# Attention and routed experts on one core: routing spread behind its batches, tables in four stages, first tile asked for earlier

## What is computed

```python
x = x + xattn(layernorm(x), ctx, ctx, Wq, Wk, Wv, Wo, bo)     # softmax(q k / 4) v Wo + bo
gate = softmax(layernorm(x) @ w_gate.T)                        # 8 experts
topk_scores, topk_idx = top_k(gate, 2)
h = gelu(einsum('td,edh->teh', ln_x, W1) + b1)
y = einsum('teh,ehd->ted', h, W2) + b2
x = x + einsum('ted,te->td', y, cw)                            # cw: the two scores, else 0
```

## Time and profile before

| | us |
|---|---|
| median of 3 runs | 514.05 (508.76 to 515.09) |
| span of the profiled execution | 496.2 |
| TensorE busy | 446.2 (90%) |
| VectorE busy | 361.9 (73%) |
| ScalarE busy | 324.5 (65%) |
| GpSimd busy | 179.4 (36%) |

### The profile page before, as it was taken

One profiled execution on the slowest core, in us unless ns is written; L12 is line 12 of the kernel. 1 busy time (PEld: TensorE's weight loads), 2 busy tenths in 40 slices (PEclk: granted clock), 3 DMA queues, 4 the chain that ended last, 5 costly groups with the idle time before them and its releaser, 6 DMA issues.

```text
span 496.2 us, 10173 instructions
## 1 busy us (share of the span) xinstructions
PE 446.2 (90%) x3585; PEld 373.5 (75%) x3585; DVE 361.9 (73%) x784; ACT 324.5 (65%) x521; POOL 179.4 (36%) x220
## 2 busy tenths in 40 slices
PE   5797989999998987858889989999999999999992
PEld 3354666767666664538889989999898898998982
DVE  4456776777777764546978997698789788797871
ACT  2133677667756633546969875898778879778860
POOL 5144340452620288701362505245321224212313
PEclk9799999999999976766999999999999999999997
DMA  7676624334122022367375999697797988977823
GB/s 235 189 208 191 205 85 155 109 127 139 66 91 85 26 77 91 131 218 306 135 239 187 282 286 248 231 281 246 227 264 234 273 259 256 279 257 243 282 37 36
DMA packets 44624, 93.19 MB, mean 188 GB/s; under 512 B 6990, under 2 KB 30350, under 8 KB 38684
## 3 DMA queue, kind: packets, MB, share of 16 engines
q1 hardware_dynamic: 35340, 81.56, 49.9%
q0 software_dynamic: 7152, 9.46, 9.6%
q10 hardware_dynamic: 2080, 1.49, 1.0%
HBM read 63.10 MB, written 14.32 MB: 156 GB/s over the span
## 4 chain that ended last, share of the span: by engine, by line
PE 55%; issue 10%; POOL 10%; DMA 8%; DVE 8%; ACT 5%; SPq 2%; ACTq 1%; DVEq 0%; POOLq 0%
PE bank L1380 14%; PE S L1344 10%; POOL lists L617 5%; PE bank L1447 5%; PE S L1357 5%; PE S L1479 4%; DVE nmax L940 3%; POOL x2n L607 3%; PE bank L1430 3%; DMA w_in<-in_W 3%; PE bank L1514 2%; PE bank L1439 2%; DMA lists<-zero 2%; PE bank L1422 2%; PE S L1502 2%
## 5 line engine op out<-in xcount | busy, mean ns | idle before, releaser
L576 POOL DMA_INDIRECT out<-y,slot x39 | 74.0, 1898 | 160.7 <-DVE y L848 87.4
L940 DVE TENSOR_REDUCE nmax<-S 128x4 f32<-128x1024 f32 x64 | 78.3, 1224 | 48.2 <-PE S L1479 45.5
L1344 PE MATMUL S<-xgT,Q 128*128 128x256 f32 x512 | 97.1, 289 | 3.2 <-DVE xgT L816 3.2
L1254 ACT ACTIVATE prob<-S 128x1024 f32<-128x1024 f32 x64 | 65.7, 1027 | 28.1 <-PE S L1502 26.4
L1344 PEld LDWEIGHTS S<-xgT,Q 128*128 128x128 f32 x512 | 79.9, 192 | 3.6 <-issue 2.5
L1158 ACT ACTIVATE hf<-S,b1c 128x256 f32<-128x256 f32 x128 | 53.2, 467 | 31.2 <-PE S L1344 30.6
L793 DVE TENSOR_TENSOR K<-w_in,Q 128x1024 fp32r<-128x1024 f32 x46 | 56.3, 1225 | 23.4 <-ACT Q L1120 23.2
L1344 PE MATMUL S<-xgT,K 128*128 128x256 f32 x256 | 72.7, 284 | 0.0
L1380 PE MATMUL bank<-W2p,hp 128*128 128x256 f32 x528 | 67.9, 285 | 0.0
L1380 PEld LDWEIGHTS bank<-W2p,hp 128*128 128x128 f32 x528 | 64.6, 191 | 0.0
L832 DVE TENSOR_TENSOR hp<-hf,hp 128x512 fp32r<-128x512 f32 x64 | 44.1, 689 | 18.9 <-ACT hp L1178 18.7
(11 more groups left out here) (205 smaller groups left out, 815.5 us busy)
## 6 DMA issues: line engine op xcount, KB each, us to landing
w_in<-in_W SPq DMA_DIRECT2D x46, 1024.0 KB, 7.2
K<-flat_k SPq DMA_DIRECT2D x24, 256.0 KB, 2.4
Q<-flat_q SPq DMA_DIRECT2D x24, 256.0 KB
xg<-lists SPq DMA_DIRECT2D x16, 265.0 KB, 5.7
b_in<-in_b SPq DMA_DIRECT2D x23, 128.0 KB, 6.2
lists<-zero SPq DMA_DIRECT2D x9, 265.0 KB, 9.0
cin<-in_ctxT SPq DMA_DIRECT2D x8, 256.0 KB, 3.3
xin<-in_x SPq DMA_DIRECT2D x8, 256.0 KB, 3.9
```

The source lines that it names most:

```text
L576: st_y[i % 4].after(pool.indirect_dma_start(out=out, out_offset=bass.IndirectOffsetOnAxis(ap=slot[i % 4][:, t:t + 1], axis=0), in_=y[i % 2 ...
L940: max_done.after(dve.tensor_reduce(nmax[n % 4][:, :, :, m].rearrange("p t r -> p r t"), S1[:].rearrange("p r (t k) -> p r t k", t=TT), AX. ...
L1254: exp_done.after(act.activation(prob[s % 4][:].rearrange("p r t l -> p (r t l)"), S2[:].rearrange("p r l -> p (r l)"), ACT.Exp, scale=SCALE))
L1344: ins = pe.matmul(h_bank[pair][:, u, 0:n], W1p[k][a][:, kc, m * P:(m + 1) * P], xgT[k][c][:, kc, 0:n], start=(j == 0), stop=(j == len(term ...
```

## The change

The reach of the first stage is cut from 5 to 3 tiles and a stage is added; groups 0 to 2 are routed earlier, batch 3's to 7's back parts shift by some steps, the experts' units begin at step 74 in place of 76, and SyncE comes to tiles 0 and 1 at step 66 in place of 71. The maxima of batch 7 are turned and copied out behind that step's scores, exponential and weighted values, no longer ahead of them. The first stage's operations are handed out 6 to a step as those of the other stages are, and not all at once.

```diff
-    SURE = (5, 2)
+    SURE = (3, 2, 2)
-    UNIT_STEP = 76
+    UNIT_STEP = 74
-    ROUTE = dict(logits=38, choose=39, gate_exp=40, gates=42, tags=46, count=50, places=51, rows=52, scatter=54)
     LATE_BACK = {
-        4: dict(div=52, divide=53, ao=54, aT=55, o=57, add=58, store=59, ln2=59, norm2=59, y=61, yT=62),
-        5: dict(div=59, divide=59, ao=60, aT=61, o=61, add=62, store=63, ln2=62, norm2=63, y=64, yT=65),
-        6: dict(div=67, divide=67, ao=68, aT=69, o=69, add=70, store=71, ln2=71, norm2=71, y=72, yT=73),
-        7: dict(div=77, divide=77, ao=79, aT=79, o=81, add=81, store=83, ln2=81, norm2=82, y=84, yT=84)}
-    LATE_ROUTE = {
-        1: dict(logits=60, choose=60, gate_exp=61, gates=62, tags=62, count=62, places=62, rows=63, scatter=63),
-        2: dict(logits=63, choose=63, gate_exp=64, gates=65, tags=65, count=65, places=65, rows=65, scatter=66),
-        3: dict(logits=66, choose=66, gate_exp=67, gates=68, tags=68, count=68, places=69, rows=69, scatter=70),
-        4: dict(logits=74, choose=74, gate_exp=75, gates=76, tags=76, count=76, places=76, rows=77, scatter=78),
-        5: dict(logits=86, choose=86, gate_exp=88, gates=88, tags=88, count=89, places=89, rows=89, scatter=90)}
-    LISTED = {0: (3, 70), 1: (4, 79), 2: (5, 92)}
+        3: dict(div=44, divide=45, ao=46, aT=47, o=48, add=49, store=50, ln2=49, norm2=50, y=51, yT=52),
+        4: dict(div=51, divide=51, ao=52, aT=53, o=53, add=54, store=55, ln2=54, norm2=55, y=57, yT=58),
+        5: dict(div=59, divide=59, ao=60, aT=61, o=61, add=62, store=63, ln2=62, norm2=64, y=67, yT=68),
+        6: dict(div=67, divide=67, ao=68, aT=69, o=70, add=71, store=72, ln2=72, norm2=73, y=75, yT=76),
+        7: dict(div=75, divide=75, ao=76, aT=77, o=78, add=78, store=79, ln2=78, norm2=79, y=81, yT=82)}
+    ROUTES = {
+        0: dict(logits=45, choose=46, gate_exp=47, gates=48, tags=48, count=48, places=49, rows=49, scatter=50),
+        1: dict(logits=53, choose=53, gate_exp=54, gates=55, tags=55, count=55, places=56, rows=56, scatter=57),
+        2: dict(logits=59, choose=59, gate_exp=60, gates=61, tags=61, count=60, places=61, rows=61, scatter=62),
+        3: dict(logits=69, choose=69, gate_exp=70, gates=71, tags=71, count=71, places=72, rows=72, scatter=73),
+        4: dict(logits=77, choose=77, gate_exp=78, gates=79, tags=79, count=79, places=80, rows=80, scatter=81),
+        5: dict(logits=83, choose=83, gate_exp=84, gates=85, tags=85, count=85, places=86, rows=86, scatter=87)}
+    LISTED = {0: (2, 62), 1: (3, 73), 2: (4, 81), 3: (5, 87)}
...
-        SP_TILES = {71: (0, 1), 76: (2,), 79: (3,), 82: (4,), 86: (5,), 90: (6,)}
+        SP_TILES = {66: (0, 1), 74: (2,), 77: (3,), 80: (4,), 84: (5,), 88: (6,)}
...
             if i == 0:
-                for n in range(1, 6):
+                for n in range(NB - len(SURE)):
                     sp.wait_ge(st_list[n % KEPT].sem, 16 * TT * TOP * (n // KEPT + 1))
                 sp.wait_ge(st_zero.sem, 16)
-            for k, n in ((1, 6),):
+            for k, n in ((1, 5), (2, 6)):
...
-        POOL_TILES = {84: 0, 88: 1, 92: 2, 96: 3}
+        POOL_TILES = {82: 0, 86: 1, 90: 2, 94: 3, 98: 4}
...
-                if "total" in now and now["total"] == 0:
-                    for _ in lists_of(0):
-                        pass
-                elif "total" in now:
+                if "total" in now:
+                    assert next(working, "done") == "done"
                     working = lists_of(now["total"])
...
-                if "mx" in now:
+                if "mx" in now and now["mx"] < NB - 1:
                     maxima_out(now["mx"])
...
                     sums_out(n, m // 2)
+                if "mx" in now and now["mx"] == NB - 1:
+                    maxima_out(now["mx"])
...
-                if "mx" in now:
+                if "mx" in now and now["mx"] < NB - 1:
                     turn_maxima(now["mx"])
...
                     weighted(n, m // 2)
+                if "mx" in now and now["mx"] == NB - 1:
+                    turn_maxima(now["mx"])
```

More of the change, by code:

```diff
@@ L140, in build @@
             due[LATE_BACK[n][name] if n in LATE_BACK else MP * n + o][name] = n
-    for i, ns in enumerate(GROUPS):
-        for name, o in ROUTE.items():
-            due[LATE_ROUTE[i][name] if i in LATE_ROUTE else MP * ns[-1] + o][name] = i
+    for i, steps in ROUTES.items():
+        for name, step in steps.items():
+            due[step][name] = i
     for stage, (i, step) in LISTED.items():
@@ L302, in build @@
         st_zero, st_x2 = signal("st_zero", 16), signal("st_x2", 16)
-        st_late = [signal(f"st_late{n}", 16) for n in range(6, NB)]
+        st_late = [signal(f"st_late{n}", 16) for n in range(NB - len(SURE), NB)]
         st_list = [signal(f"st_list{i}", 16) for i in range(KEPT)]
@@ L490, in store @@
                 sp.wait_ge(*emptied_at("o", n))
-                (st_x2 if n < 6 else st_late[n - 6]).after(sp.dma_start(out_d[n], x2[:, n * TT:(n + 1) * TT]))
+                (st_x2 if n < NB - len(SURE) else st_late[n - NB + len(SURE)]).after(sp.dma_start(out_d[n], x2[:, n * TT:(n + 1) * TT]))
             def empty_rows():
@@ L569, in add_to_output @@
             else:
-                pool.wait_ge(st_x2.sem, 16 * 7)
+                pool.wait_ge(st_x2.sem, 16 * (NB - len(SURE) + 1))
             for k in range(len(SURE)):
@@ L1106, in dve_attention @@
                 if s >= UNIT_STEP:
-                    for _ in range(LIST_OPS if s < LISTED[2][1] else LIST_OPS // 2):
+                    for _ in range(LIST_OPS if s < LISTED[3][1] else LIST_OPS // 2):
                         next(working, None)
```

## The result

The change makes the kernel slower: 520.81 us (518.87 to 523.58, 4 runs) against 512.59 us (508.76 to 515.09, 4 runs), ratio 1.0167 with an interval of 1.0111 to 1.0222. The forecast was 503.05 with a range of 494 to 512. The profiled execution took 522.24 us with a span of 520.9.

What follows compares the result with a forecast made beforehand. The experts' part, from 250 us, was taken as bound by TensorE's own work, so only the stretch before could move: -1.0 - 3.1 - 8.2 + 1.3 = -11.0 us, from 514.05 to 503.05 us, range 494 to 512.

Steps and rivals of the forecast that it cites:

- steps 48 to 55: Attention steps that take in 5.0 us of moved TensorE work: 24.5 to 25 us in place of 20.01, +4.7.
- steps 56 to 63: Attention steps that lose the same 5.0 us; VectorE is next, 19 us for 17 of work: -5.5.
- to the end of batch 6's o: From step 63's end to batch 6's output projection: the 2.62 us wait goes, 17.0 us after 20.1, -3.1.
- o to u0: Batch 6's output projection to unit u0: rows and weights covered, VectorE's queue sums to 10.1 us after 18.3, -8.2.
- u0, sum of these: Start of the experts' first unit: its first matmul at about 214, before at 225.35.
- u0 to the end: Experts' units to the span's end: 270.85 us carried as constant, +1.3 for VectorE's added work in u0 to u7.
- one more small count product: nothing, it hides under units: In the experts' units: an added small count product costs nothing.
- the last table 3 steps earlier and the same 8 clearing DMAs: nothing: The 64.15 us to tile 7: the earlier last table and unchanged clearing DMAs add nothing.
- 17.85 us: Distance of the runs' median above the traced span, added to the forecast span of 485.2 us.
- the rival of the slower kernel: Steps 56 to 73 too thin for TensorE, half clock from step 58 to u0: +4.9, 519 us; chance 0.10.
- The later point that holds the end: Tiles 5 to 7 paced by transfers, from 253 to 317: all but 2 us given back, 512 us; chance 0.10.
- The crowding of the small DMA: Tile 0 and 1 transfers delay the DMA of batch 7's maxima: step 66 5.5 us late, 508.5; chance 0.13.

Runs made afterwards that it cites:

- a_ends: The changed kernel with the eight clearing DMAs asked for behind tile 5's first weights, not tile 6's; ratio 1.0115 to the kernel before.
- the three repairs: The changed kernel with batch 6's y and yT one step earlier, two count products one step later, clearing behind tile 5's first weights; 498.43 us, ratio 0.9994.
- best_again: Second measurement of the three repairs plus tile 0's first weights split a step earlier and the second table begun in step 74; 498.66 us, ratio 0.9976.
- b_again: The kernel before, unchanged, run and profiled a second time; ratio 0.9978 to the kernel before.
- a_tot: The changed kernel with the count products for the third and fourth table one step later (82 and 88); ratio 1.0095 to the kernel before.
- a_copy4: Probe on the three repairs: ScalarE copies group 4's logits in place of their exponential, so batch 6's gates are wrong; ratio 1.0017 to the kernel before.
- a_split: The changed kernel with the second half of groups 0 and 1's scatters three steps later in GpSimd's program, group 2's at step 63; 523.74 us.

## Why the prediction was wrong

The forecast was a sum from the earlier trace rows on, so its steps are judged first on traces of the same kind, without late releases: the first trace of before against a_ends, which up to u0 is the changed kernel. Busy time by stretch, a_ends, cut as the prediction cut it:

```profile
143.59:170.84 27.25, 22.76 (x234) 16.69 (x230) 21.11 (x59) 14.45 (x22) 16.75 (x17) 1.00 0.26 90
170.84:189.90 19.06, 16.12 (x182) 10.46 (x178) 16.18 (x55) 12.23 (x18) 11.89 (x13) 1.00 0.28 94
189.90:207.80 17.90, 13.63 (x108) 9.00 (x108) 5.74 (x28) 9.06 (x14) 3.57 (x4) 0.81 0.67 237
207.80:219.77 11.97, 4.43 (x56) 2.48 (x55) 8.80 (x38) 6.71 (x9) 4.44 (x4) 0.90 0.33 127
```

| step of the prediction | forecast | measured |
|---|---|---|
| ahead of step 48 | 0 | +1.1 |
| steps 48 to 55 | +4.7 | +7.2 (27.25 - 20.01) |
| steps 56 to 63 | -5.5 | -5.4 (19.06 - 24.43) |
| to the end of batch 6's o | -3.1 | -2.2 (17.90 - 20.10) |
| o to u0 | -8.2 | -6.4 (11.97 - 18.34) |
| u0, sum of these | -12.3 | -5.6 |
| u0 to the end | +1.3 | +16.4 (287.2 - 270.85) |

**Steps 48 to 55.** TensorE's work was right to 0.04 us (22.8 forecast, 22.76 measured). The wait above it was carried over as 2.2 us and is 4.5: VectorE goes from 14.74 to 21.11 us busy, its choice of group 1 stands behind logits that stand behind an output projection, and the next maximum behind that. An engine's busy time was added and not the turns that the two engines now take. The half clock went as forecast: 1.00 in both lines, against the earlier trace rows.

**Steps 56 to 63.** The time is right, its parts less so: TensorE was to be busy for 14.1 us and was for 16.12. VectorE's 17 us of work were 16.18, and the 19 us for the stretch came to 19.06. With TensorE's share 2 us off, the fit of the sum is in part luck.

**To the end of o, and o to u0.** Sizes only. The queue of VectorE that was summed to 10.1 us takes 12.0, with VectorE busy for 8.80 of it; the first weights were hidden (asked for at 208.4 in the changed kernel's trace, split by VectorE from 224.2 on), and TensorE waits 5.3 us in place of 4.

**From u0 on.** This is the step that failed: "TensorE's own work, which this change leaves alone", carried as 270.85 and +1.3. It came to +16.4. The term for VectorE's work held, if anything: with the causes of the stops removed, u0 to u8 takes 28.73 us against 28.00. What was not in it are the stops, each a single operation that the change puts one step too near to its input or one place too late in a queue: bank reuse in step 75, the products in steps 81 and 87, the clearing. Nor was the half clock in it that comes with a stop. The removal of each cause alone gives 3.3, 6.1 and 5.1 us of span in single traces, all three give 11.3, and the time then equals the kernel before. The bank of step 75 the prediction didn't look at. It did look at the other two ("one more small count product: nothing, it hides under units", "the last table 3 steps earlier and the same 8 clearing DMAs: nothing") and priced them by their length and not by what they wait for; the counts of these two tables stood 3 steps behind `places` before and stand 1 behind after, which the diff shows.

**The base.** 17.85 us were taken for time outside the span. But for 1.3 us they were, by all that the traces show, the difference between an execution without late releases and runs with them. It didn't enter the forecast of the difference, since it was added back; but rows of a 497.5 us execution were used for a kernel whose runs take 508 to 515. Some slips of the working changed nothing: +4.7 and -5.5 are -0.8, not -1.0; 24.7 and 25 us for steps 48 to 63 are +5.3, not +5.7, in the rival of the slower kernel; the half clock of the earlier trace rows adds up to 37.6 us, where "over 32" was written; and slices 2 and 40 of the earlier trace rows show a lower clock as well.

**The rivals.** It got slower, but not by the path of the rival that said so. Half clock throughout steps 56 to 73 did not come: with late releases the granted clock is 0.87 and 0.83 there, without them 1.00 and 0.81. The later point that holds the end was right in its place (idle TensorE between u16 and u28, the clearing), and wrong in its mechanism and price: not a pace of transfers that gives the gain back, but a new stop that takes more than was won. The crowding of the small DMA did not come: TensorE waits 1.9 to 2.2 us for it in step 66, in a_ends its first scores are at 194.8, 4.9 us behind the last maximum, where 4.3 was forecast. The Trainium skill (DMA: Bandwidth & Descriptors, section Issuing engines are not separate DMA queues) says that DMAs run on the same 16 DMA engines and interleave, whichever engine starts them. A case that fits comes later: where the clearing is asked for ahead of tile 6's rows, TensorE waits for these rows, 1.8 us in a_ends, 3.43 in the three repairs, 5.17 in best_again. In best_again the DMA engines' busy share is 1.06 to 1.13 from 270 to 295; that the clearing, and not the weights beside it, holds the rows up isn't shown.

**The late releases** are not why the change is slower. b_again loses 239.1 - 225.4 = 13.7 us to u0 against the first trace, the changed kernel 233.7 - 219.8 = 13.9 against a_ends: about the same, in other places. The ratio of the changed kernel itself in a set without them was not measured; a_tot and a_ends, each with one stop less, lie at 1.0095 and 1.0115 there.

## What to carry to other kernels

A forecast that moves the start of a bound stretch must also walk through that stretch: for every operation that the new order puts into it, ask what it reads, how many steps ahead of it that is made on an engine that runs later, and which bank or queue place it takes. A stretch that is "TensorE at nine tenths" can lose more to a few short waits, and to the half clock behind them, than its start wins. And profile the kernel before a second time: the first trace may not be of the kind that its times are. For the same reason a probe is to be read against a partner of the same kind: against the wrong one, a_copy4 seemed to win nothing.

## What the chip showed that was not expected

In four of six sets of runs, engines were released up to 10.9 us late while GpSimd issued scatters one behind another. Most of the long ones ended 1.4 to 2.3 us behind the last scatter of a run, shorter ones within a run, some in runs of four. In the other two sets the same kernels with the same runs of scatters (8, 8 and 4) had none, and neither had the first trace of before with 16 in a row. They go with about 14 us more of span, and with medians of 514 against 499 us for the kernel before. What differs between the sets is not known, only that one chip gave both kinds. Whether a run's length matters is open too: the edits that parted the scatters fell into sets without late releases. Beside this, a scatter edit in program order is no edit in time: in a_split GpSimd ran through its list as before, since nothing made it wait.
